# Gated stack, first stage: upper product of one batch laid beside the lower product of the one in front

## What is computed

```
def _smooth_quant_linear(x, w):
    amax_x = jnp.max(jnp.abs(x), axis=0)
    amax_w = jnp.max(jnp.abs(w), axis=0)
    s = jnp.sqrt(jnp.maximum(amax_x, EPS) / jnp.maximum(amax_w, EPS))
    xs = x / s
    ws = w * s
    x_scale = jnp.maximum(jnp.max(jnp.abs(xs), axis=-1, keepdims=True), EPS) / QMAX
    w_scale = jnp.maximum(jnp.max(jnp.abs(ws), axis=-1, keepdims=True), EPS) / QMAX
    x_q = jnp.clip(jnp.round(xs / x_scale), -QMAX, QMAX)
    w_q = jnp.clip(jnp.round(ws / w_scale), -QMAX, QMAX)
    return x_q @ w_q.T * x_scale * w_scale.T
h = _smooth_quant_linear(xe, guw)          # "upper", 512 -> 512
gate, up = jnp.split(h, 2, axis=-1)
a = jax.nn.silu(gate) * up
... _smooth_quant_linear(a, dw)            # "lower", 256 -> 512
x = x + jnp.tanh(g_xattn[0]) * _L0_xattn_ref(_layernorm(x, axis=-1), fside_BxS2xS2_0, ctx_1024)
```

## Time and profile before

| | us |
|---|---|
| median of 3 runs (1462.79 to 1468.9) | 1463.84 |
| the profiled execution | 1463.91 |
| its span | 1462.3 |
| busy TensorE, VectorE, ScalarE, GpSimd | 1181.6, 864.6, 649.3, 389.5 |
| first stage, to the first row of the next | 300.7 |
| in it busy TensorE, VectorE, ScalarE, GpSimd | 179.1, 193.8, 92.1, 92.6 |

### The profile page before, as it was taken

How to read it: one execution, slowest core, us unless ns; L and a number is a source line. 1 busy time by engine, 2 the same in 40 slices (tenths; PEclk the granted TensorE clock), 3 DMA queues, 4 the chain that set the end, 5 groups by cost and what they waited for, 6 DMA issues and landing times. The chain is left out here.

```text
span 1462.3 us, 16858 instructions
## 1 busy us (share of the span) xinstructions
PE 1181.6 (81%) x5253; PEld 516.5 (35%) x5317; DVE 864.6 (59%) x1321; ACT 649.3 (44%) x1143; POOL 389.5 (27%) x467
## 2 busy tenths in 40 slices
PE   2657575769996999996346998999899999985897
PEld 2333333345553444443101222322232222232453
DVE  3585858561242555531579888677777777415634
ACT  1332333445541222223235766566666666643543
POOL 0505050511013222211333432222222330005332
PEclk9777877889998999999566999999999999997999
DMA  5131402153424444432771333222232221007011
GB/s 201 44 123 37 142 23 106 58 188 116 158 87 150 152 140 148 146 119 104 227 180 48 99 110 93 85 70 85 69 95 83 70 75 32 2 0 87 29 41 47
DMA packets 106355, 141.56 MB, mean 97 GB/s; under 512 B 20788, under 2 KB 75572, under 8 KB 106280
## 3 DMA queue, kind: packets, MB, share of 16 engines
q1 hardware_dynamic: 87432, 111.37, 23.7%
...
## 5 line engine op out<-in xcount | busy, mean ns | idle before, releaser
L2265 DVE TENSOR_REDUCE a_top<-PS 128x2 f32<-128x1024 f32 x256 | 308.4, 1223 | 95.4 <-PE PS L2026 91.4
L2112 ACT ACTIVATE a_E<-PS 128x512 f32<-128x512 f32 x512 | 277.6, 596 | 149.7 <-PE PS L2009 146.5
L2009 PE MATMUL PS<-a_Q,a_K 99*128 99x512 bf16 (+1 forms) x469 | 157.3, 386 | 16.6 <-ACT a_E L2112 6.2
L2026 PE MATMUL PS<-a_K,a_Q 64*128 64x512 bf16 x512 | 104.2, 405 | 48.9 <-DVE a_top L2265 26.7
L1251 PE MATMUL PS<-f_W,f_GT 128*128 x312 | 142.3, 599 | 0.0
L2039 PE MATMUL PS<-a_E,a_V 128*32 128x512 f32 x1024 | 136.8, 606 | 0.4 <-ACT a_E L2112 0.4
L2009 PEld LDWEIGHTS PS<-a_Q,a_K 99*128 99x128 bf16 (+1 forms) x512 | 44.2, 97 | 155.5 <-ACT a_E L2112 103.5
L1642 POOL TENSOR_TENSOR a_qf<-a_qf,a_tab 128x512 f32<-128x512 f32 x15 | 19.0, 1268 | 269.9 <-DVE a_swapped L2209 269.9
L1307 DVE TENSOR_TENSOR f_H<-f_SG,PS 128x256 f32<-128x256 f32 x39 | 16.4, 421 | 125.8 <-ACT f_SG L1291 125.8
L1251 PEld LDWEIGHTS PS<-f_W,f_GT 128*128 128x128 f32 x312 | 57.1, 193 | 57.6 <-issue 57.6
L1954 PE MATMUL PS<-a_xT,a_wq 128*128 128x512 f32 x128 | 74.0, 675 | 2.1 <-ACT a_xT L2082 0.8
...
## 6 DMA issues: line engine op xcount, KB each, us to landing
f0r_raw<-in_L_ffn_W_dram SPq DMA_DIRECT2D x24, 512.0 KB, 5.1
...
v_units<-V SPq DMA_DIRECT2D x16, 512.0 KB, 3.7
a_V<-v_units SPq DMA_DIRECT2D x16, 512.0 KB, 3.7
...
```

The lines of the kernel that those rows point to most:

```text
L2009: nc.tensor.matmul(PS[:, 4 + h % 2, :], K6[k][0:rows_, o, head // 2, kt * P:(kt + 1) * P], Q6[k][0:rows_, o, head // 2, :], start=True, st ...
L2026: last = nc.tensor.matmul(PS[:, 2 * pair + o, :], Q6[k][at, o, h // 2, t * P:(t + 1) * P], K6[k][at, o, h // 2, :], start=True, stop=True)
L2112: nc.scalar.activation(E[step % 2][:, h, :], PS[:, 4 + h % 2, :], ACT.Exp).then_inc(exp_done, 1)
L2265: nc.vector.tensor_reduce(top[:, h - h % 2:h - h % 2 + 2, t], PS[:, 2 * pair:2 * pair + 2, :], AX.X, ALU.max).then_inc(maxed, 1)
```

## The change

The stage is one unrolled run of five iterations. Iteration `i` holds the upper linear of batch `i` and the lower of batch `i - 1`, their steps interleaved on every engine by hand; the first has only an upper, the last only a lower.

- PSUM: `up` has banks 0 to 3, `down` 4 to 6, the side jobs bank 7 (before, both linears had 0 to 3 and up, and the side jobs 5). Upper transposes go by halves of two banks, weights and then activations, and VectorE reduces each half, in four instructions of 2 banks in place of two of 4; the lower weights and activations pass through banks 4 and 5, one after the other. The fourth lower product takes bank 4 again, once its first `y` is out.
- The outputs of the upper product are taken first (`take_up`), then those of the lower (`take_down`).
- `xqT` is copied by ScalarE, behind `wqT`. The s rows go out in two signals, that of the weights first.
- tanh(g) is multiplied into the lower row scales (`gated_scale`), so `y` comes out gated, and X is added by GpSimd, four instructions behind the angles of the next batch; the last batch's are VectorE's.
- Side jobs no longer belong to the iteration of their batch: they stand in one list, of which an iteration takes 1, 0, 3, 2 and 2 into its five slots, with the angle job of batch `i` in the second. Three stand between the row of upper weight scales and that of the lower, two between the turned upper and the turned lower quantized rows.
- At the start, the context, positions and Wkv are loaded ahead of `dw` and the gates; TensorE's wait for Wkv stands at the first key product, the tanh at the end of ScalarE's first iteration, and the wait for the second load of `X` at the statistics of batch 1. Context and positions have a semaphore each.

The core of the diff:

```diff
-        up = Linear("_up", D, xh, guw, (0, 4, 0, 1, 2, 6, 4))
-        down = Linear("_down", I0, a, dw, (0, 2, 0, 1, 2, 3, 4))
+        gated_scale = sb("gated_scale", [P, 4])
+
+        up = Linear("_up", D, xh, guw)
+        down = Linear("_down", I0, a, dw)
+        assert up.kc == 4 and down.kc == 2
+        DOWN_AT = (4, 5, 6, 4)
...
+            side.sync_start(sp)
             sp.dma_start(dw[:], ctx_v[0]).then_inc(down.w_loaded, 16)
             sp.dma_start(gates[:, 0:2], g_xattn.partition_broadcast(P)).then_inc(gates_loaded, 16)
             sp.dma_start(gates[:, 2:4], g_ffn.partition_broadcast(P)).then_inc(gates_loaded, 16)
-            side.sync_start(sp)
             sp.dma_start(X[:, TB:, :], x_v[:, TB:, :]).then_inc(x_loaded[1], 16)
...
-            with sp.Fori(1, NB) as b:
-
...
+            for i in range(NB + 1):
+                side.sync_store(sp, i, 0)
+                if i < NB - 1:
+
+                    sp.wait_ge(up.scales_ready, i + 1)
+                    sp.dma_start(guw[:], fside_v[i + 1]).then_inc(up.w_loaded, 16)
+                if 1 <= i < NB:
+
+                    sp.wait_ge(down.scales_ready, i)
+                    sp.dma_start(dw[:], ctx_v[i]).then_inc(down.w_loaded, 16)
+                side.sync_store(sp, i, 1)
...
-            side.pool(pool)
...
+            for b in range(NB):
+                side.pool_angles(pool, b)
+                if b:
+                    for t in range(TB):
+                        pool.wait_ge(y_ready, (b - 1) * TB + t + 1)
+                        rows = X[:, (b - 1) * TB + t, :]
+                        nc.gpsimd.tensor_tensor(rows, y[:, t, :], rows, ALU.add).then_inc(x_updated, 1)
+                side.pool_tables(pool, b)
...
-                pe_linear(pe, b, up, (0, 1, 2, 3), first)
-                pe_linear(pe, b, down, (4, 5, 6, 7), first)
-                side.tensor_end(pe, b)
...
+            for i in range(NB + 1):
+                u, d = i, i - 1
+                if u < NB:
+                    pe.wait_ge(up.w_loaded, 16 * (u + 1))
+                    for half in range(2):
+                        if u:
+                            pe.wait_ge(hs_ready, (u - 1) * TB + 2 * half + 2)
+                        turn_w(up, u, half, 2 * half)
+                    if u == 0:
+                        side.tensor_start(pe)
+                    if d >= 0:
+                        pe.wait_ge(down.w_loaded, 16 * (d + 1))
+                        if d:
+                            pe.wait_ge(y_ready, d * TB)
+                        turn_w(down, d, 0, 4)
+                    pe.wait_ge(up.x_ready, u + 1)
+                    for half in range(2):
+                        pe.wait_ge(up.reduced, 4 * u + half + 1)
+                        turn_x(up, u, half, 2 * half)
+                else:
+                    pe.wait_ge(down.w_loaded, 16 * (d + 1))
+                    pe.wait_ge(y_ready, d * TB)
+                    turn_w(down, d, 0, 4)
+                if d >= 0:
+                    pe.wait_ge(down.reduced, 2 * d + 1)
+                    pe.wait_ge(down.x_ready, (d + 1) * TB)
+                    turn_x(down, d, 0, 4)
+                if u < NB:
+                    s_rows(up, u, (0, 0), (1, 0))
+                side.tensor(pe, i, 0)
+                if d >= 0:
+                    s_rows(down, d, (6, 0), (6, 256))
+                side.tensor(pe, i, 1)
+                if u < NB:
+                    wsc_row(up, u, 1)
+                side.tensor(pe, i, 2)
+                if d >= 0:
+                    wsc_row(down, d, 4)
+                if u < NB:
+                    pe.wait_ge(up.wq_ready, u + 1)
+                    turn_quantized(up, up.wq, 2, up.wqT_done)
+                    pe.wait_ge(up.wsc_row_ready, u + 1)
+                    pe.wait_ge(up.xq_ready, u + 1)
+                    turn_quantized(up, up.xq, 0, up.xqT_done)
+                side.tensor(pe, i, 3)
+                if d >= 0:
+                    pe.wait_ge(down.wq_ready, d + 1)
+                    turn_quantized(down, down.wq, 5, down.wqT_done)
+                    pe.wait_ge(down.xq_ready, d + 1)
+                    turn_quantized(down, down.xq, 6, down.xqT_done)
+                if u < NB:
+                    pe.wait_ge(up.wqT_ready, u + 1)
+                    pe.wait_ge(up.xqT_ready, u + 1)
+                    for t in range(TB):
+                        product(up, t, t)
+                if d >= 0:
+                    pe.wait_ge(down.wsc_row_ready, d + 1)
+                    pe.wait_ge(down.wqT_ready, d + 1)
+                    pe.wait_ge(down.xqT_ready, d + 1)
+                    for t in range(TB - 1):
+                        product(down, t, DOWN_AT[t])
+                side.tensor(pe, i, 4)
+                if d >= 0:
+                    pe.wait_ge(y_ready, d * TB + 1)
+                    product(down, TB - 1, DOWN_AT[TB - 1])
...
-            v.wait_ge(L.xqT_done, b + 1)
-            nc.vector.tensor_copy(L.xqT[:], PS[:, L.bxq:L.bxq + L.kc // 2, :].bitcast(BF16)
-                                  .rearrange("p a (c n) -> p (a c) n", n=512)).then_inc(L.xqT_ready, 1)
...
+            for i in range(NB + 1):
+                u, d = i, i - 1
+                if d >= 0:
+                    side.scalar(act, d, 4)
+                    side.scalar_waves(act, d)
+                    for t in range(TB):
+                        act.wait_ge(hs_ready, d * TB + t + 1)
+                        nc.scalar.activation(silu_g[:, t, :], hs[:, t, 0:I0], ACT.Silu).then_inc(silu_ready, 1)
+                if u < NB:
+                    root(up, u)
+                if d >= 0:
+                    root(down, d)
+                side.scalar(act, i, 0)
+                side.scalar(act, i, 1)
+                if u < NB:
+                    shift_w(up, u)
+                    take_wsc_row(up, u, 1)
+                side.scalar(act, i, 2)
+                if d >= 0:
+                    shift_w(down, d)
+                    take_wsc_row(down, d, 4)
+                if u < NB:
+                    take_turned(up, u, up.wqT, 2, up.wqT_done, up.wqT_ready)
+                    take_turned(up, u, up.xqT, 0, up.xqT_done, up.xqT_ready)
+                side.scalar(act, i, 3)
+                if d >= 0:
+                    take_turned(down, d, down.wqT, 5, down.wqT_done, down.wqT_ready)
+                    take_turned(down, d, down.xqT, 6, down.xqT_done, down.xqT_ready)
+                if u < NB - 1:
+                    norm_root(u + 1)
+                if u == 0:
+                    act.wait_ge(gates_loaded, 32)
+                    nc.scalar.activation(tg[:], gates[:], ACT.Tanh).then_inc(tg_ready, 1)
+            side.scalar(act, NB, 4)
...
+                    nc.vector.tensor_tensor(a[:, t, :], silu_g[:, t, :], hs[:, t, I0:], ALU.mult).then_inc(down.x_ready, 1)
...
+                ch.step(nc.vector.tensor_scalar(gated_scale[:], down.scale[:, 0:4], tg[:, 0:1], None, ALU.mult))
...
+            def take_down(b, last):
+                v.wait_ge(down.wsc_row_ready, b + 1)
+                if b:
+                    v.wait_ge(x_updated, b * TB)
...
+                    nc.vector.scalar_tensor_tensor(y[:, t, :], PS[:, DOWN_AT[t], :], gated_scale[:, t:t + 1], down.wsc_row[:],
+                                                   ALU.mult, ALU.mult).then_inc(y_ready, 1)
+                    if last and t:
+                        add_rows(b, t - 1)
+                if last:
+                    add_rows(b, TB - 1)
+
+            def add_rows(b, t):
+                v.wait_ge(y_ready, b * TB + t + 1)
+                rows = X[:, b * TB + t, :]
+                nc.vector.tensor_tensor(rows, y[:, t, :], rows, ALU.add).then_inc(x_updated, 1)
...
+            for i in range(NB + 1):
+                u, d = i, i - 1
+                if u < NB:
+                    reduce_turned(up, u, 0, 0)
+                    reduce_turned(up, u, 1, 2)
+                if d >= 0:
+                    reduce_turned(down, d, 0, 4)
+                if u < NB:
+                    v.wait_ge(up.x_ready, u + 1)
+                    reduce_turned(up, u, 2, 0)
+                    reduce_turned(up, u, 3, 2)
+                if d >= 0:
+                    gate(d)
+                if u < NB:
+                    ratio(up, u)
+                    s_columns(up, u)
+                if d >= 0:
+                    reduce_turned(down, d, 1, 4)
+                    ratio(down, d)
+                if u < NB:
+                    scale_w(up, u, 1, 0)
+                if d >= 0:
+                    s_columns(down, d)
+                if u < NB:
+                    w_scales(up, u)
+                    x_scales(up, u, 0, 0)
+                if d >= 0:
+                    v.wait_ge(down.x_ready, (d + 1) * TB)
+                    scale_w(down, d, 6, 256)
+                    w_scales(down, d)
+                if u < NB:
+                    quantize_w(up, u)
+                    quantize_x(up, u)
+                if d >= 0:
```

(33 more changed lines are left out.)

444 lines of the change are left out of this document (196 added, 248 removed).

## The result

The changed kernel took **1401.06 us** (median; 1398.27 to 1401.94) beside 1463.32 of the kernel before: a ratio of 0.956, interval 0.9536 to 0.959. The forecast was 1427, with a range from 1403 to 1449, so the kernel is 2 us faster than the lower end of the range. The profiled span is 1396.6 us instead of 1462.3.

A forecast was written before the change was run, and what follows sets the result against it. It took the first stage's serial batches, chains walking from engine to engine, as the bound. 57 + 57 + 57 + 54.5 + 34 = 259.5 instead of 296.3: 1463.9 - 36.8 = 1427 us, range 1403 to 1449.

The forecast's parts named there:

- The start: Before the first joint iteration: loads waited for later, upper part alone; joint work starts at 57 us, 53 without blocking.
- The joint iterations: Upper part of one batch beside lower of another: 57, 57 and 54.5 us, set by VectorE's chain with GpSimd's blocking.
- The walk: Joint iteration: VectorE and GpSimd operations wait for each other's end; quantizing down ends at 47.0 instead of 35.5, iteration +6.6.
- The mark: Sign in the profile after: VectorE's 128x512 xs steps in joint iterations at a mean near 1 us instead of 0.48.
- the 50.4 of the ping-pong: Joint iteration without blocking: side products and their copies alternate through one PSUM bank, 2.66 us each; 50.4 us.
- The iteration without blocking: Joint iterations with shorter context transposes and no GpSimd blocking: 47.7, 49.1 and 47.7 us.
- The tail: Last iteration, lower part alone, GpSimd idle: 34 us to the last V copy.
- Costed at nothing: First stage: SP's store order, the four X additions, unrolled loops and table loads given no cost.
- (a): GpSimd hardly blocks VectorE's quantizing; single-bank side jobs set joint iterations: end 231.5, 235 with lower clock, 1403 us; chance 0.17.
- (b): Key and value products stay at 1.2 GHz, or handoffs come later: 1450 us; chance 0.24 together with (d).
- (c): GpSimd's angle chain takes over, delaying sines, SiLU and gate: 73 us an iteration, 1475 us; chance 0.04.
- (d): Some wait, as on PSUM banks, ties both parts together: 9 us more each iteration, 1454 us; chance 0.24 with (b).

The follow-up runs named there:

- experiment 4: Kernel before with only the start's edits (load order, later Wkv wait, tanh and wait for X's second load): 1454.70 us, ratio 0.9944.
- experiment 1: Changed kernel without GpSimd's angle arithmetic, only the two clips of a batch left: 1391.05 us, ratio 0.9498.
- experiment 2: Changed kernel with GpSimd's angle chain replaced by five steps of the 1.93 us kind and the clip for each half: 1396.89 us.
- experiment 3: Changed kernel with the additions into X back on VectorE instead of GpSimd: 1403.43 us, ratio 0.9589.
- the two edits of 5: Changed kernel with side-job stores ahead of dw's reload wait, 1402.77 us; fourth side-job slot ahead of xq_up's turn, 1403.47; both, 1404.50.
- (7): Changed kernel with xs_up's scaling moved from VectorE to ScalarE: 1409.32 us; with xs_down's scaling moved too: 1417.24 us.

## Why the prediction was wrong where it was

**What bounded the kernel before: right.** The SiLU wait is hidden (34.5 to 1.1 us), and the whole difference lies in the first stage.

**The start: 57 was 51.4.** xh was to be done at 12.2 and the reductions at 18.4; they were at 13.2 and 18.0. The start's own gain, 10.5 by my terms (28.9 to 18.4), was 11.8 in the profiled execution of experiment 4 and 8.2 by its medians. Two terms in it were too dear. The angle product was to take 3.8 us at the lower clock and took 2.07. And xq_up, which I had at 41 beside GpSimd and 35.7 without it, ended at 38.0. Of the 4 us that blocking was to cost there nothing is seen at the last side product: it ends at 51.4 with GpSimd's angle work and at 52.8 without.

**The joint iterations: 57, 57 and 54.5 were 48.5, 51.1 and 46.2**, and this is the step that failed: "I walk the two queues in turn, each operation waiting for the end of the one that holds". The walk delayed VectorE by 11.5 us. From the groups above, against the same operations without the angle work (xs_up 481, xh 542, xs_down 347, xq_down 695, the two lower scale steps 170 each): 1.7 + 0.3 + 0.7 + 0.9 + 0.8 = about 4.5 us. VectorE's busy time says the same: 4.6, 4.7 and 4.4 us more in the three iterations than in experiment 1. The mean of xs_up that I named as a mark, near 1 us, was almost met (914 ns). At the start xs_up goes in turn with GpSimd's steps just as I walked it (0.84, 1.50, 0.85, 1.50 us); in the joint iterations the fourth runs free (0.47), inside a step of 1.93 us. The mark said nothing about the other half of the walk, which was the 1.93 us steps (experiment 2) and most of the lower part.
The second half of the same step is the sum: 11.5 on VectorE was to give 6.6 at the end, with 4.6 hidden under the wait for the root. Of the 4.5 really lost 1.0 to 2.8 reach the end of an iteration in the profiled executions (experiment 1). Had I put 4.5 into my own walk, it would have ended at the 50.4 of the ping-pong. Of the 29 us between my 259.5 and the 230.5, the three iterations are 22.7, the start is 5.6 and the tail 0.8.

**The iteration without blocking: too long as well.** I gave 47.7, 49.1 and 47.7. Cut as I cut them, at the end of the last side product, the kernel without GpSimd's angle work shows 43.5, 50.1 and 45.1: 5.8 us less in all. VectorE's own work, which I had at 45 to 47 us, is 41.4 there in the second iteration, the one that from hs to hs holds all of it. I had the first side product and the angle product of an iteration at the lower clock; at 111.80 and 115.44 in iteration 2 they took 1.88 and 2.06 us, the clock 1.00 in both. Iteration 2 alone is over its floor; a late store explains 0.5 of that, where I had allowed 1.

**The tail: 34 was 33.2. Costed at nothing:** the four additions on GpSimd do hide (VectorE's next reductions run beside them), and moving them there is worth 2.4 to 4.4 us (experiment 3). The order of the outputs, which I had not priced apart, is worth 5.4.

**The rivals.** (a), the blocking that hardly binds, gave 231.5 for the end, to which I added 3.5 for the clock: the end was 230.5. I gave it 0.17 because I took a few rows of full blocking as a rule for all of GpSimd's steps, though they are of different kinds. Its mechanism is true only by half: the blocking is there, but a good part of it falls where VectorE would wait anyway. That its number is met within 1 us is partly luck: it leaves out the blocking, which costs 5.4 us at the end in the profiled executions, and its iterations without blocking are 5.8 us too long. (b) holds in single products (3.66 us at 118.28, behind a wait of only 0.17, and 3.72 at 83.55) and not for the run of them. (c) is refuted: GpSimd's work, 25.1 us long (68.72 to 93.86), is done before the sines are asked for. (d) is refuted by the windows. The range's lower end was (a) with its allowance of 3.5 us for the clock, and nothing stood below it: the allowance was not needed, and the plain (a) would have given about 1399.

The Trainium skill, page "SBUF — State Buffer", section "SBUF: two separate sides", has the pair of ports that VectorE and GpSimd share held "for the whole instruction". The trace agrees for GpSimd's additions (xs_up 1.50 us) and for VectorE's wq_up against a GpSimd step (0.62 became 1.67). It does not agree for the steps of 1.93 us: xs_up was held by at most 0.37 us, and xq_up ran for 1.2 us inside one. By the rule, as I walked it, the iteration was to be 57; the measurement decides.

**What sets an iteration now.** The runs fit two chains of nearly the same length, VectorE's and that of the side jobs. Adding 2.5 us to VectorE costs 0.8 to 1.5 (3), taking 4.5 off it gains 1.0 to 2.8 in the profiled executions (1); adding 2.6 us to ScalarE amid the side jobs costs up to 5.5 in an iteration (7). TensorE's side products and ScalarE's copies pass through one PSUM bank in turn, and in the runs with a long hold-up there the products behind it ran at the lower clock. That this chain would be faster with a second bank is argued, not shown: all eight banks are taken, and it wasn't tried. The second iteration is 3.6 to 5.8 us longer than its neighbours with and without GpSimd's work. From hs to hs it alone holds both the y of the iteration in front and the statistics and xh of the next batch: VectorE is busy 46.1 us in it, 43.3 and 41.0 in the others. That covers its distance from the third and leaves 1.2 to 3 us of its distance from the first open; the late store is 0.5, and the two edits of 5 together took 2.1 off it without a gain in the whole.
